# Second attention of a four-stage kernel: which operand stands in TensorE, and where the softmax sums are divided

## What is computed

```python
q = (x @ Wq + bq).reshape(B, N, NUM_HEADS, HEAD_DIM)      # 16 heads of 16, x normed before
k = (y @ Wk + bk).reshape(B, M, NUM_HEADS, HEAD_DIM)      # y: the context, 128 rows
v = (y @ Wv + bv).reshape(B, M, NUM_HEADS, HEAD_DIM)
scores = jnp.einsum('bnhd,bmhd->bhnm', q, k) * scale
attn = jax.nn.softmax(scores, axis=-1)
out = jnp.einsum('bhnm,bmhd->bnhd', attn, v).reshape(B, N, IMAGE_DIM)
h = jax.nn.relu(out @ W1 + b1)
return h @ W2 + b2
```

## Time and profile before

| | us |
|---|---|
| median of 3 runs | 757.74 |
| the three runs | 754.29, 757.74, 759.83 |
| span of the profiled execution, first to last instruction | 754.8 |
| TensorE matmul busy | 647.9 (86%) |
| TensorE weight load busy | 453.4 (60%) |
| DVE busy | 363.4 (48%) |
| ACT busy | 221.8 (29%) |
| POOL busy | 180.9 (24%) |

### The profile page before, as it was taken

The page is one execution under the profiler, slowest core; times in us unless marked ns, Lnnn a source line. Parts: engine busy times, 40 slices in busy tenths (PEclk is TensorE's granted clock), DMA queues, the critical chain, the costliest instruction groups (busy, mean ns, idle before and its releaser), DMA issues.

```text
span 754.8 us, 10099 instructions
## 1 busy us (share of the span) xinstructions
PE 647.9 (86%) x3506; PEld 453.4 (60%) x3507; DVE 363.4 (48%) x844; ACT 221.8 (29%) x361; POOL 180.9 (24%) x151
## 2 busy tenths in 40 slices
PE   4978689999799998899996996319999999999993
PEld 3747457686467786466873675214666666666662
DVE  4334548647558557477373667462322232223220
ACT  1232045621444432356213431002222222222210
POOL 2100222001312003221012210041444444444422
PEclk9977799999899999899998999557999999999997
DMA  9900100001200003000007020201223222322221
GB/s 358 416 9 22 56 1 1 1 22 43 69 0 0 21 0 111 0 0 0 0 23 283 1 85 0 60 8 37 43 46 51 45 42 44 51 46 42 44 34 22
DMA packets 20759, 40.31 MB, mean 53 GB/s; under 512 B 3872, under 2 KB 17440, under 8 KB 19456
## 3 DMA queue, kind: packets, MB, share of 16 engines
q1 hardware_dynamic: 8736, 25.16, 8.8%
q0 software_dynamic: 7488, 10.39, 8.4%
q10 hardware_dynamic: 4512, 4.46, 1.8%
HBM read 30.37 MB, written 9.64 MB: 53 GB/s over the span
## 4 chain that ended last, share of the span: by engine, by line
PE 70%; issue 10%; DVE 8%; ACT 4%; POOL 2%; DVEq 2%; DMA 2%; POOLq 0%; ACTq 0%
PE ps L613 34%; PE ps L945 18%; PE ps L617 9%; PE ps L962 8%; POOL var_xh L304 1%; ACT ring L480 1%; DVE mx L1124 1%; DMA out_x<-OT,row_no 1%; DVEq L1037 1%; DVE ring L1128 1%; POOL ring L361 1%; DVE rc L1134 1%; DVE XH L1005 1%; DVE experts L1036 1%; ACT experts L404 1%
## 5 line engine op out<-in xcount | busy, mean ns | idle before, releaser
L945 PE MATMUL ps<-experts,keep 128*128 x312 | 143.1, 602 | 0.3 <-issue 0.3
L375 POOL DMA_INDIRECT out_x<-OT,row_no x39 | 61.7, 1583 | 129.5 <-ACT OT L592 123.7
L945 PEld LDWEIGHTS ps<-experts,keep 128*128 128x128 f32 x312 | 57.3, 194 | 58.3 <-issue 58.3
L1398 DVE SCALAR_TENSOR_TENSOR keep<-keep,row_w,ps 128x512 f32<-128x512 f32 x39 | 29.2, 750 | 109.8 <-PE ps L945 109.8
L304 POOL TENSOR_TENSOR var_xh<-var_xh,minus_half 128x4 f32<-128x4 f32 x16 | 16.9, 1059 | 252.0 <-DVE var_xh L1000 252.0
L962 PE MATMUL ps<-experts,keep 128*128 x312 | 73.9, 380 | 1.8 <-DVE keep L1402 1.8
L962 PEld LDWEIGHTS ps<-experts,keep 128*128 128x128 f32 x312 | 59.1, 190 | 26.0 <-issue 19.9
L613 PE MATMUL ps<-experts,keep 128*128 128x256 f32 (+1 forms) x184 | 70.2, 533 | 4.8 <-DVE experts L1064 1.7
L1124 DVE TENSOR_REDUCE mx<-ps 128x8 f32<-128x1024 f32 x32 | 39.0, 1220 | 55.6 <-PE ps L613 55.6
L613 PE MATMUL ps<-ring,V 128*32 128x128 f32 x512 | 64.0, 278 | 1.5 <-DVE OT L1136 1.5
L613 PE MATMUL ps<-ring,keep 128*32 128x128 f32 x512 | 63.5, 273 | 0.0
(11 more groups left out here) (204 smaller groups left out, 954.7 us busy)
## 6 DMA issues: line engine op xcount, KB each, us to landing
experts<-in_experts SPq DMA_DIRECT2D x8, 1536.0 KB, 16.5
keep<-in_keep SPq DMA_DIRECT2D x1, 3075.0 KB, 19.1
ring<-in_fold SPq DMA_DIRECT2D x1, 2112.0 KB, 10.9
experts<-in_x SPq DMA_DIRECT2D x4, 512.0 KB, 3.4
experts<-in_ctxT SPq DMA_DIRECT2D x4, 512.0 KB, 3.8
out_x<-X ACTq DMA_DIRECT2D x4, 512.0 KB, 3.1
normed<-XH ACTq DMA_DIRECT2D x4, 512.0 KB, 4.0
experts<-in_ctx SPq DMA_DIRECT2D x4, 384.0 KB, 3.3
```

Of the source, the lines that this page charges most:

```text
L375: pool.indirect_dma_start(out=out_d, out_offset=bass.IndirectOffsetOnAxis(ap=row_no[:, t:t + 1], axis=0), in_=YO[t % DEEP], in_offset=None ...
L945: ins = pe.matmul(ps[:, 2 * (r % 2) + g, :], XIT[r % 2][:, k, :], experts[:, bass.ds(at + (2 * k + g) * INTER, INTER)], start=(k == 0), st ...
L1398: dve.scalar_tensor_tensor(HA[r % 2], HA[r % 2], row_w[r % DEEP][:, 0:1], ps[:, 2 * (r % 2) + 1, :], ALU.mult, ALU.mult).then_inc(act_ok, 1)
```

## The change

`attend1` makes eight matmuls a unit, one for each head: the turned probabilities of the head (`PQ`, 128x128) stand, and 17 columns stream, 16 of values and one of ones. So the output has the query rows on partitions and for each head 16 sums and the sum of its probabilities, 272 columns of one bank for a batch. V1 is set to ones once, and each group's values are copied between the ones (`VS`). `divide` runs once a batch: a reciprocal of the 16 sums of each row and one product into `heads_out`. Two turns (`turn_heads`) and a copy by ACT (`heads_turned`) bring the result to OT as before. `hidden1` is called in two parts with `turn_heads` of the fourth batch between them. Banks: `attend_bank` gives a batch bank 7, or 0 for the fourth batch in the loop, and 2 and 7 in turn in the last group. `ones_half` and the two tiles `rc` go.

```diff
+        HV = HD + 1
+        VS = V1.rearrange("p t o n -> p (t o n)")[:, 0:GB * NH * HV].rearrange("p (t h n) -> p t h n", t=GB, h=NH)
...
-        rc = [sb(f"rc{n}", [P, P]) for n in range(2)]
+        head_sum = sb("head_sum", [P, NH])
+        heads_out = sb("heads_out", [P, D])
...
-        def attend_bank(u):
-
-            return 7 if u < UNITS - 1 else 0
+        def attend_bank(b, last):
+
+            if last:
+                return 2 if b % 2 else 7
+            return 7 if b < GB - 1 else 0
...
-            pool.memset(V1[:, :, :, :], 0.0).then_inc(v1_zero, 1)
+            pool.memset(V1[:, :, :, :], 1.0).then_inc(v1_set, 1)
...
-                for o in range(2):
-                    half = lambda v: v.rearrange("p t (h n) -> p t h n", n=32)[:, :, :, o * HD:(o + 1) * HD]
-                    ins = act.copy(half(V1[:, :, o, :]), half(halves(5)))
-                ins.then_inc(s["v1"], 1)
+                act.copy(VS[:, :, :, 0:HD], halves(5).rearrange("p t (h n) -> p t h n", n=HD)).then_inc(s["v1"], 1)
...
+            def heads_turned(n, b, last=False):
+                act.wait_ge(s["oT_ps"], GB * n + b + 1)
+                act.copy(OT[:, :, b * S:(b + 1) * S], split(bank(attend_bank(b, last))[:, 0:D], KD)).then_inc(s["ot"], 1)
...
-                for u in (2, 3, 4):
-                    exp1(n, u)
-                    probs1_turned(n, u)
+                exp1(n, 2)
+                probs1_turned(n, 2)
+                exp1(n, 3)
+                heads_turned(n, 0)
+                probs1_turned(n, 3)
+                exp1(n, 4)
+                probs1_turned(n, 4)
                 rows2_turned(n + 1)
                 exp1(n, 5)
+                heads_turned(n, 1)
                 probs1_turned(n, 5)
...
                 probs1_turned(n, 7)
+                heads_turned(n, 2)
+                heads_turned(n, 3)
                 hidden1(n)
...
                 probs1_turned(LAST, u)
+                if u >= 3 and u % 2:
+                    heads_turned(LAST, u // 2 - 1, last=True)
+            heads_turned(LAST, GB - 1, last=True)
             exp_gate(0, B - GB)
...
-            def attend1(n, u):
+            def attend1(n, u, last=False):
                 bb, t = u // 2, u % 2
                 pe.wait_ge(s["pt"], UNITS * n + u + 1)
-                if 0 < u < UNITS - 1:
-                    pe.wait_ge(s["ot"], UNITS * n + u)
-                for st in range(4):
-                    out = ps[32 * st:32 * st + 32, attend_bank(u), :]
-                    mm(out[:, 0:S], [(V1[:, bb, o, 32 * (4 * t + st):32 * (4 * t + st) + 32], PQ[u % 2][:, 2 * st + o, :]) for o in range(2)])
-                    ins = mm(out[:, S:2 * S], [(kept("ones_half", 2)[:, o, :], PQ[u % 2][:, 2 * st + o, :]) for o in range(2)])
+                if not t and bb and attend_bank(bb, last) == attend_bank(bb - 1, last):
+                    pe.wait_ge(s["ot"], GB * n + bb)
+                if not t and last and bb >= 2:
+                    pe.wait_ge(s["ot"], GB * n + bb - 1)
+                for h in range(HT8):
+                    at = (HT8 * t + h) * HV
+                    ins = mm(bank(attend_bank(bb, last))[:, at:at + HV], [(PQ[u % 2][:, h, :], VS[:, bb, HT8 * t + h, :])])
                 ins.then_inc(s["ot_ps"], 1)
...
+            def turn_heads(n, b, last=False):
+                pe.wait_ge(s["on"], GB * n + b + 1)
+                for k in range(KD):
+                    ins = turn(bank(attend_bank(b, last))[:, k * P:(k + 1) * P], heads_out[:, k * P:(k + 1) * P])
+                ins.then_inc(s["oT_ps"], 1)
...
                 score1(n, 4)
+                turn_heads(n, 0)
                 turn_probs1(n, 3)
...
                 score1(n, 6)
+                turn_heads(n, 1)
                 turn_probs1(n, 5)
...
                 turn_probs1(n, 7)
+                turn_heads(n, 2)
                 attend1(n, 6)
                 attend1(n, 7)
-                hidden1(n)
+                hidden1(n, slice(0, GT - S))
+                turn_heads(n, 3)
+                hidden1(n, slice(GT - S, GT))
                 slot_inputs(n + 1)
...
                 turn_probs1(LAST, u)
+                if u >= 3 and u % 2:
+                    turn_heads(LAST, u // 2 - 1, last=True)
                 if u:
-                    attend1(LAST, u - 1)
-            attend1(LAST, UNITS - 1)
-            hidden1(LAST)
+                    attend1(LAST, u - 1, last=True)
+            attend1(LAST, UNITS - 1, last=True)
+            hidden1(LAST, slice(0, GT - S))
+            turn_heads(LAST, GB - 1, last=True)
+            hidden1(LAST, slice(GT - S, GT))
...
-            def divide(n, u):
-                bb, t = u // 2, u % 2
-                dve.wait_ge(s["ot_ps"], UNITS * n + u + 1)
-                o = attend_bank(u)
-                dve.reciprocal(rc[u % 2][:, :], bank(o)[:, S:2 * S])
-                settle()
-                dve.tensor_tensor(OT[:, t, bb * S:(bb + 1) * S], bank(o)[:, 0:S], rc[u % 2][:, :], ALU.mult).then_inc(s["ot"], 1)
+            def divide(n, b, last=False):
+                dve.wait_ge(s["ot_ps"], UNITS * n + 2 * b + 2)
+                o = bank(attend_bank(b, last))[:, 0:NH * HV].rearrange("p (h n) -> p h n", h=NH)
+                dve.reciprocal(head_sum[:, :], o[:, :, HD])
+                settle()
+                dve.tensor_tensor(heads_out.rearrange("p (h n) -> p h n", h=NH), o[:, :, 0:HD],
+                                  head_sum[:, :].unsqueeze(2).broadcast_to([P, NH, HD]), ALU.mult).then_inc(s["on"], 1)
```

More of the change, by code:

```diff
@@ L42 @@
 KEEP, KEEP_N = columns([
-    ("ident", P), ("ones", P), ("ones_half", 2 * 32), ("head_mask", HT4), ("half_mask", 2),
+    ("ident", P), ("ones", P), ("head_mask", HT4), ("half_mask", 2),
     ("ln1_g", KD), ("ln1_b", KD), ("ln2_g", KD), ("ln2_b", KD), ("bq", KD), ("bv", KD),
@@ L209, in build @@
                  "xh3 xb xT3_ps xT3 k_ps k v1_ps v1 q1_ps q1 f_ps f y_ps xh4 xT4_ps xT4 gl_ps gl "
-                 "kb sc_ps sub exp pt_ps pt ot_ps ot")
+                 "kb sc_ps sub exp pt_ps pt ot_ps on oT_ps ot")
         names += "".join(f" var_{m} rs_{m}" for m in norms)
@@ L213, in build @@
         fold_ps, fold_ok = sem("fold_ps"), sem("fold_ok")
-        v1_zero, half_set = sem("v1_zero"), sem("half_set")
+        v1_set, half_set = sem("v1_set"), sem("half_set")
         blank_set, hot_ok, placed = sem("blank_set"), sem("hot_ok"), sem("placed")
@@ L517, in _ @@
             act.dma_start(xh_d[B * S:B * S + P, :], blank[:, :]).then_inc(stored, 16)
-            act.wait_ge(v1_zero, 1)
+            act.wait_ge(v1_set, 1)
             act.wait_ge(fold_ok, 2)
@@ L783, in outputs1, with hidden1 @@
+            def hidden1(n, own):
+                pe.wait_ge(s["ot"], GB * (n + 1) - (0 if own.stop == GT else 1))
+                for m in range(H1 // P):
+                    ins = mm(bank(3 + m)[:, own], [(kept("aW1", KD)[:, k, m * P:(m + 1) * P], OT[:, k, own]) for k in range(KD)])
+                    if own.stop == GT:
+                        ins.then_inc(s["f_ps"], 1)
             def outputs1(n, half):
@@ L1272, in _ @@
                 shift(n, 2)
-                divide(n, 0)
                 over_sum(n + 1)
@@ L1276, in _ @@
                 add_attention(n + 1)
-                divide(n, 1)
+                divide(n, 0)
                 gather_stats("xh2")
@@ L1280, in _ @@
                 norm(n + 1, X0, XH0, D, "xh2")
-                divide(n, 2)
                 shift(n, 5)
-                divide(n, 3)
+                divide(n, 1)
                 shift(n, 6)
-                divide(n, 4)
                 shift(n, 7)
                 top(n + 1)
-                divide(n, 5)
-                divide(n, 6)
-                divide(n, 7)
+                divide(n, 2)
+                divide(n, 3)
                 shares(n + 1)
@@ L1305, in _ @@
                 shift(LAST, u, 0 if u % 2 else 3)
[L1306 to L1309, removed]
+                if u >= 3 and u % 2:
+                    divide(LAST, u // 2 - 1, last=True)
+            divide(LAST, GB - 1, last=True)
             route(0, B - GB)
@@ L1445 @@
     col = lambda w: tiles(w.reshape(-1, 1))[:, :, 0]
-    half = np.zeros((P, 2, 32), np.float32)
-    half[:, 0, :HD] = 1
-    half[:, 1, HD:] = 1
     keep = packed(KEEP, KEEP_N, {
-        "ident": np.eye(P, dtype=np.float32), "ones": np.ones((P, P), np.float32), "ones_half": half,
+        "ident": np.eye(P, dtype=np.float32), "ones": np.ones((P, P), np.float32),
         "head_mask": np.tile(np.kron(np.eye(HT4, dtype=np.float32), np.ones((HD, 1), np.float32)), (2, 1)),
```

## The result

The changed kernel takes 775.92 us (median of 6 runs, 767.29 to 778.0), the kernel before 755.25 us over the runs taken with it. The ratio is 1.0313, with a 95% interval of 1.0202 to 1.0423: slower, where TensorE has less to do in attend1 and DVE much less. This ratio and all later ones compare means and leave out, as slow, the runs of a kernel that lie more than 1.5% above its fastest; the medians of all runs here give 1.027.

A forecast was written before the change was run, and what follows sets the result against it. The prediction took TensorE to bound the kernel. Work and waits, -8.4 us, plus clock, +27.5 us, gave +19.1 us and a forecast of 776 us; the range was 749 to 795 us.

The forecast's parts named there:

- attend1's unit drops from 2.39 us to the loads' pace: On TensorE: weight loads set the time of a unit of 16 records, 1.73 us, bounds 1.70 and 2.4.
- The waits: New TensorE waits per loop pass: 0.95 us by turn_heads(0), 0.4 at turn_probs1(7), 0.6 by turn_heads(3); old waits save 1.0.
- The loop pass's work and waits: Each of three loop passes: less attend1 work, added turns, old and new waits, -2.6 us (bounds -4.5 to -0.5).
- The last group: After the loop: exp_gate waits behind heads_turned(3), so DVE's route takes the end from TensorE; only 0.4 us is gained.
- The clock: TensorE's clock falls in attention's thin streams, mainly at group ends, costing 27.5 us, bounds 0 and +60.
- The fall ahead of the pair: Clock falls shortly before attend1(6) and (7) at a group's end, slowing them, turns and hidden1's start: together 7 us.
- Clock: +27.5 us: Clock cost over all groups: 20 us at the groups' ends and 7.5 us in the middles of three passes.
- Work and waits together: -8.4 us: Three loop passes at -8 us and the last group's 0.4 us, before any change of TensorE's clock.
- the first rival: The clock holds throughout attention, so only work and waits count: -8.4 us, 749 us; chance 0.2.
- the fresh loads are slow: Rival: attend1's loads from buffers ACT just wrote take 2.2 us a unit, without a clock fall: 765 us; chance 0.05.
- it falls only at the ends, and mostly late: Rival: clock falls only at the four groups' ends, costing 2 to 4 us each: 757 to 765 us; chance 0.2.
- it stays low through most of the attention: Rival: nothing in attention is wide enough to restore the clock, +50 to 60 us: about 800 us; chance 0.1.

The follow-up runs named there:

- the two half-wide runs: The changed kernel with 64 columns streamed only in units 5 to 7 of each group (749.68 us), or only in units 0 to 4 (753.72 us).

## Why the prediction was right, and where its sum was not

The forecast was 776 us, slower; measured are 775.92 us. Point by point:

- TensorE bounds the kernel and attend1's unit drops from 2.39 us to the loads' pace: right, 1.71 us against 1.73.
- The waits: 0.95, 0.36 and 0.46 us against 0.95, 0.4 and 0.6; right.
- The loop pass's work and waits: the two kernels' second passes, from gate_logits to gate_logits, are 190.4 to 294.8 (104.4 us) before and 184.6 to 285.9 (101.3 us) with 64 columns, each with one low stretch near its start. So the work gives 3.1 us a pass, where the forecast had 2.6: inside its bounds.
- The last group: route takes the end from TensorE, as forecast, and moving exp_gate out of its way gave 1.65 us in place. The 0.4 us put as the gain there was not measured by itself.
- The clock: the direction, the cause (thin streams on a TensorE that is busy nearly all the time) and the place (the end of each group, and the middle of a pass) were right. The fall ahead of the pair, the dearer of its two places, is the one seen in the second and third pass and the last group. The pair at the low level, 6.7 us against 3.52, is 3.2 of the 3.5 us forecast. The size was not: at the same work, 64 columns against 17 are worth 775.9 - 735.3 = 41 us, and the step "Clock: +27.5 us" was too small. Most of the gap is the middle of the passes: put at 7.5 us for three passes, at a chance of a third for each of two stretches, and worth 15 us (41 less the 26 of the ends) to 22 (taken alone). The ends were put at 20 us and are worth 21 to 26. In the profile of the changed kernel the middle is low in two passes of three (227 to 234, 332 to 343 us); in that of the kernel with exp_gate moved, which at 779.8 us is nearer to most runs, in all three (127 to 138, 236 to 247, 345 to 356). There the passes take 10.8, 8.1 and 10.6 us more than with 64 columns, where the forecast's clock had 7.3.
- The step that failed together with it is "Work and waits together: -8.4 us" taken as all that the change gives when the clock holds. With the clock up the kernel takes 735 us, not the first rival's 749. The passes' work gives 9.3 of the 19 us below the kernel before; most of the rest lies in low stretches of the kernel before that the 64-column kernel's profile does not have (near 306, 401 and 415 us; its one fall between the start and the routing is near 194), as the next interval, 99.3 us (285.9 to 385.2) against 105.5 (294.8 to 400.3), shows. Another 2.6 us arose ahead of the loop, where the two kernels do the same work (the loop's first turns start at 86.30 us before, at 83.66 with 64 columns). I took those falls as fixed. The two errors, 41 - 27.5 = 13.5 us too few on the clock and 19.1 - 8.4 = 10.7 us too little gain without it, nearly cancel. The forecast also started from a median of 757.74 us, which more runs brought to 755.25: the difference was put at 18 us and is 21. So the total was hit more closely than its terms were, and that closeness is luck.
- Three readings were off without moving the sum by more than 1 us. The mean of 7 and 2 us is 4.5, not 4.8. "The clock never fell within attention" overlooked the last group: behind a wait of 2.85 us the turns at 415.37 ran at the low level, 1.97 us for eight. And that only wide matmuls end a low stretch does not hold: the clock came back at 233.5 us behind 16 turns, and with four matmuls added the scores of 512 columns in the last group's low stretch from 419 us did not end it before 446.

What stays open: whether thin streams alone would bring the clock down. In the profile of the changed kernel the falls of the second pass and the one at the end of the last group each come behind a wait of about 1 us; the kernel with 64 columns shows that such waits alone do not do it, and no run has 17 columns without the waits. Open too is whether those other falls went because of the earlier wide attends or because the passes came to lie otherwise in time. Three more kernels with 64 or 128 columns in every unit also show a single fall in the loop, which speaks for more than luck, but no run separates the two. It is also not shown how the clock's two prices divide among single groups; the two half-wide runs don't add up.

The rivals: that the clock holds fell with the first profile, that the fresh loads are slow with the 1.71 us. That it falls only at the ends, and mostly late, fell too: the middles fell as well, and the total is above its 757 to 765 us. That it stays low through most of the attention did not happen in the loop passes, where 214 to 223.5 and most of 231 to 247 ran at the high level; the last groups of the two kernels with added matmuls came near it, with 27 and 28 us low at a stretch.

The Trainium skill, page "TensorE: Matmul & The Clock Gate", section "Why this matters for your kernels", asks for TensorE to be kept busy and free of long idle gaps. The windows disagree for thin streams: 0.50 over 10 us in which TensorE was busy in all of them and its loads in 9.60.

## What to carry to other kernels

When an edit swaps which operand stands, count not only the time of the loads and streams but also how many columns stream behind each load, and read PEclk beside the busy time: here the pair ran at 0.50 while the profile had TensorE busy for 10.00 of 10.00 us. If the loads set the pace, stream more columns than are needed up to the point where they cost time, and let later writes cover the rest; here 64 columns for 17 turned a kernel 3% slower than the one before into one 2.6% faster. Where runs of one kernel spread by their clock, judge an edit of a microsecond or two in place, from one mark of the trace to another.

## What was not expected of the hardware

With 32 columns the clock still fell in the middle and at the end of two passes, with 64 in neither; between the two kernels lie 31 us. And useless matmuls can pay: two that stood behind a stretch that had already lost the clock were no gain (779 us in the one run that counts), four that began ahead of it came with 765 us, against 776 us without any.
